# Moving the z projection of a graph attention layer into its edge softmax, with picks in two phases

## The chip, the cores and the metric

The kernel runs on 1 core of a Trainium2 chip. The metric is the device time of one execution in microseconds, as the median over runs. A program of several thousand lines of Python writes every engine's instruction stream by hand, with semaphores between engines.

## The reference

One forward pass over a graph of 3750 nodes with 512 features and 60000 edges sorted by destination: a graph attention layer, an expert-choice mixture of experts, a second graph attention layer and a top-2 mixture of experts, each on a layer norm of x and with x added back. Only the attention layers matter here. Layer 0, with 8 heads of 64:

```
z = einsum('ni,hoi->nho', h, Wfc)
s_src = einsum('nho,ho->nh', z, a_src); s_dst = einsum('nho,ho->nh', z, a_dst)
e = leaky_relu(s_src[src] + s_dst[dst])
ex = exp(e - segment_max(e, dst)[dst])
alpha = ex / segment_sum(ex, dst)[dst]
out = segment_sum(alpha[:, :, None] * z[src], dst)
```

Layer 1 is the same with another slope, e times (1 + et_emb[edge_type]) times the edge weight, and a maximum of at least zero.

## The kernel before, in words

Each attention layer is a stage `front`, which makes z and the edge weights alpha, and a stage `aggregate`, which gathers z rows by edge and sums them. `front` consists of two blocks; a block is one instruction stream for each engine with a barrier of all engines at its end, and `aggregate` starts after another.

**First block, entry.** There are NT = 30 tiles of 128 nodes. SP loads x in five batches of six tiles (`load_x`, L296 to L311) and the weights. VectorE takes statistics of a batch (`stats`, L407), normalises it into two slots (`norm`, L416 to L423) and multiplies the weights with the attention vectors (L431, L432), which gives `wa`. TensorE turns each tile (`turn`, L577), ACT copies it out with two copies (L723, L724) into `edge` and `alpha`, and TensorE makes the scores of source and destination for four tiles at a time (`score`, L585), which it turns back (L598). The scores are split into three bf16 parts (`table`, L449). The scores are also stored to HBM (`src_scores`, L335).

**First block, z.** TensorE projects the 30 tiles with eight matmuls each (L633), ACT copies each out of PSUM (L735), and SP stores it (L358). In layer 0 TensorE also counts, between the tiles, how many edges each node has, from one-hot operands that VectorE makes (L496, L497, L613), and from this come the first edge of each node (L507 to L513). In layer 1 it spreads the edge kinds (L607), which VectorE takes into `wide` (L525).

**First block, picks.** The edges are padded to 61440 and lie in `e` as 16 chunks by 8 heads over the partitions and 15 blocks of 256 edges along the free dimension. Of these blocks, ten get their source scores on TensorE: a pick is 512 edges of one chunk. VectorE makes a one-hot of the key of each edge (L551), TensorE selects with six bf16 matmuls (L674), VectorE masks by tile (L560), and two fp32 matmul records (L683) add the result into one of five PSUM banks. There are 16 x 5 = 80 picks. A row of keys and one of tiles, broadcast to 128 partitions, serves the five picks of a chunk; SP loads them into two slots (`load_rows`, L339). The other five blocks are gathered by POOL, 32 indirect transfers each (`pick`, L373), and turned on TensorE (L664). The destination scores are scattered by POOL to the first edge of each node (L395), read back by ACT in 15 blocks with two transfers each (`load_dst`, L702), turned (L664) and copied out by ACT (L748). TURNS_AT gives the pick before which each block is turned. PICKS_BEFORE gives how many gathered blocks POOL does ahead of its scatters. In layer 0, VectorE also does between picks the counting for the tables of `aggregate` (L472, L475, L476) and the run bounds (`make_bounds`, L458): two compares, two scans, four scalings. At the end come the matmuls of the tables (L690, L691) and ACT's copies of the five sums (L753).

**Second block, edge softmax.** It is a chain on VectorE of five segmented scans over 3840 columns (L787, L803) with passes between them. Each scan needs two small answers of TensorE (L900, L904) to carry over the chunks. ACT makes the flags (L877), the exponentials and the logarithm (L882, L887, L891). Then TensorE turns the weights (L911) and VectorE and ACT copy them into `alpha` (L770). TensorE's stream has nothing else here.

The order on every queue is the order of the program text; nothing is planned at run time.

## Time and profile before

| | |
|---|---|
| runs | 3551.01 us median of 3 (3549.84 to 3555.11) |
| the profiled execution | span 3551.1 us |
| PE busy | 2856.0 us, 80% |
| DVE busy | 2086.8 us, 59% |
| ACT busy | 659.4 us, 19% |
| POOL busy | 1666.6 us, 47% |

The page gives the profiled execution as a span alone. PE is TensorE's matmuls, PEld its weight loads, DVE is VectorE, ACT ScalarE, POOL GpSimd, SP SyncE. A share of the span is an average over stages with different limits, so the stages are read one by one. In the trace, "front_early" and "front_edge" are buffers of the stage `front`, "bank" is PSUM. PEclk is the clock that TensorE was granted, 1.00 being 2.4 GHz. In a timeline row "x8" is the number of instructions merged into it.

### The profile page before, as it was taken

Reading aid. Unit: us, or ns where it says so; the run is one execution under the profiler, and the core shown is the slowest. Engines: PE = TensorE matmul, PEld = TensorE weight load, DVE = VectorE, ACT = ScalarE, POOL = GpSimd, SP = SyncE. Lnnn points to the kernel's source line nnn. Section 1 sums busy time; section 2 is a strip of 40 time slices with the busy share of each in tenths; the row PEclk is TensorE's granted clock in tenths of the full one; section 3 lists DMA queues with packets and bytes.
Section 4 is the critical chain, followed back from the end, with each engine's and each line's share of the span. In section 5 each row is a group of like instructions: output and inputs, shape, how many; then the busy total and the mean of one; then the engine's idle time right before and its main releaser. Section 6 shows DMA issues by size and latency. Waiting matters only on the chain. (4 is left out here: it accounts for less than half of the span.)

```text
span 3551.1 us, 38041 instructions
## 1 busy us (share of the span) xinstructions
PE 2856.0 (80%) x9200; PEld 1383.1 (39%) x9201; DVE 2086.8 (59%) x3517; ACT 659.4 (19%) x1150; POOL 1666.6 (47%) x1601
## 2 busy tenths in 40 slices
PE   5988818888887884299999499990888898784998
PEld 2444402222222553255554244550322223273665
DVE  5778786666665876723332321559666666576554
ACT  2100110000001662011111121001211111161333
POOL 0678007777774000134443137710677777501665
PEclk9999959999998885599999799995999999956999
DMA  4226307777775112045555533720677777545666
GB/s 162 85 89 110 123 5 209 209 209 210 209 209 154 63 66 104 14 115 144 144 145 135 142 83 91 169 90 0 179 210 210 211 211 210 168 178 168 125 125 107
DMA packets 329743, 496.57 MB, mean 140 GB/s; under 512 B 175457, under 2 KB 181073, under 8 KB 328951
## 3 DMA queue, kind: packets, MB, share of 16 engines
q0 software_dynamic: 118528, 313.64, 34.7%
q1 hardware_dynamic: 83367, 176.98, 14.1%
q10 hardware_dynamic: 127696, 4.06, 2.0%
q8 instruction: 79, 1.29, 0.2%
q14 instruction: 73, 0.60, 0.1%
HBM read 407.83 MB, written 86.70 MB: 139 GB/s over the span
## 5 line engine op out<-in xcount | busy, mean ns | idle before, releaser
L994 POOL DMA_INDIRECT aggregate_zg<-z_rows,src_groups x940 | 892.0, 949 | 619.9 <-POOLq L2282 334.1
L1067 PE MATMUL bank<-aggregate_zg,aggregate_onehot 128*128 x1888 | 947.2, 627 | 122.2 <-DVE aggregate_zg L1037 115.5
L1037 DVE TENSOR_TENSOR aggregate_zg<-aggregate_zg,bank 128x1024 f32<-128x1024 f32 x470 | 573.6, 1220 | 429.5 <-DMA aggregate_zg<-z_rows,src_groups 429.1
L1067 PEld LDWEIGHTS bank<-aggregate_zg,aggregate_onehot 128*128 128x128 f32 x1888 | 304.4, 189 | 763.3 <-issue 751.0
L378 POOL DMA_INDIRECT front_d<-src_scores,src_chunks x320 | 325.1, 1016 | 188.4 <-issue 97.2
L1702 POOL DMA_INDIRECT exp_xg<-hn_rows,exp_gather_tok x64 | 71.9, 1123 | 497.1 <-DVE exp_gather_tok L1764 375.7
L674 PE MATMUL bank<-front_w,front_table 128*120 128x512 bf16 x960 | 243.7, 391 | 27.6 <-DVE front_w L551 27.6
L977 ACT ACTIVATE acc<-bank 128x512 f32<-128x512 f32 x60 | 35.8, 597 | 1084.4 <-PE bank L1067 1084.4
L1846 PE MATMUL bank<-exp_w,exp_h_t 128*117 128x512 f32 x512 | 225.7, 595 | 0.7 <-ACT exp_h_t L1793 0.7
L1713 POOL DMA_INDIRECT x_rows<-exp_y,exp_add_tok x64 | 136.5, 2133 | 165.1 <-DVE exp_y L1755 129.8
L1838 PE MATMUL bank<-exp_xg_t,exp_w 128*128 128x468 f32 x512 | 206.1, 561 | 0.7 <-ACT exp_xg_t L1782 0.7
L674 PEld LDWEIGHTS bank<-front_w,front_table 128*120 128x120 bf16 x960 | 130.6, 137 | 175.6 <-issue 94.7
L1015 DVE TENSOR_TENSOR aggregate_onehot<-bank,columns 128x256 f32<-128x256 f32 x472 | 192.1, 416 | 0.0
L683 PE MATMUL bank<-front_z,spread 120*128 120x512 f32 x320 | 168.7, 609 | 0.1
L633 PE MATMUL bank<-front_w,front_edge 128*128 128x512 f32 x360 | 166.7, 599 | 0.0
L1838 PEld LDWEIGHTS bank<-exp_xg_t,exp_w 128*128 128x128 f32 x512 | 98.2, 192 | 107.0 <-issue 107.0
L1754 DVE TENSOR_TENSOR exp_y<-bank,exp_b 117x512 f32<-117x512 f32 x64 | 44.1, 690 | 154.7 <-PE bank L1846 154.7
L1846 PEld LDWEIGHTS bank<-exp_w,exp_h_t 128*117 128x117 f32 x512 | 90.3, 181 | 114.2 <-issue 112.7
L900 PE MATMUL bank<-front_cc,head_sel 128*8 128x32 f32 x20 | 2.8, 231 | 159.4 <-DVE front_cc L789 120.2
L2103 POOL DMA_INDIRECT out_x<-exp_y,exp_slot_rows x66 | 104.5, 1584 | 49.8 <-SPq L2092 20.7
L2097 POOL DMA_INDIRECT exp_xin<-routed_rows,slot_tokens x66 | 64.4, 976 | 124.2 <-DVE exp_x_t L2124 66.8
L2182 PE MATMUL bank<-exp_w,exp_x_t 128*128 x528 | 120.5, 386 | 1.6 <-DVE exp_x_t L2124 1.6
(429 smaller groups left out, 3756.2 us busy)
## 6 DMA issues: line engine op xcount, KB each, us to landing
exp_w<-in_L_ffn_w SPq DMA_DIRECT2D x32, 1024.0 KB, 7.3
z_rows<-front_z SPq DMA_DIRECT2D x60, 256.0 KB, 2.0
aggregate_zg<-z_rows,src_groups POOLq DMA_INDIRECT x940, 3.7
front_early<-src_key SPq DMA_DIRECT2D x16, 640.0 KB, 3.8
front_early<-src_tile SPq DMA_DIRECT2D x16, 640.0 KB, 3.9
front_edge<-src_key SPq DMA_DIRECT2D x16, 640.0 KB, 3.9
front_edge<-src_tile SPq DMA_DIRECT2D x16, 640.0 KB, 4.0
exp_w<-in_L_ffn_W SPq DMA_DIRECT2D x2, 4096.0 KB, 17.4
```

What stands on the lines that cost most here:

```text
L378: pool.indirect_dma_start(picked[:, at:at + H], None, k.src_scores[:, :], bass.IndirectOffsetOnAxis(k.src_chunks[:, n:n + 1], 0)).then_inc ...
L633: mm = nc.tensor.matmul(k.ps[3 + n % 2][:, :], hn_t(c, slice(n * P, (n + 1) * P)), w[:, c, :], start=(c == 0), stop=(c == KC - 1))
L674: mm = nc.tensor.matmul(k.ps[5 + m % 2][0:HT * H, :], parts[:, part, half, :], onehot[:, m % OH, half, :], start=(part == 0 and half == 0) ...
L683: nc.tensor.matmul(sums[b], k.spread[0:HT * H, at:at + P], masked[0:HT * H, (m - 1) % 2, :], start=(c == 0), stop=(c == CH - 1)).then_inc( ...
L994: pool.indirect_dma_start(zg[:, r, j, :], None, k.z_rows[:, :], bass.IndirectOffsetOnAxis(k.src_groups[:, n:n + 1], 0)).then_inc(gathered[ ...
L1015: v.tensor_tensor(onehot_at(n), lanes.unsqueeze(1).to_broadcast([P, J, P]), bcast_last(k.columns[:, n, :], P), ALU.is_equal).then_inc(oneh ...
L1037: v.tensor_tensor(z, z, bcast_last(scales[:, at:at + J * H], DH), ALU.mult).then_inc(msg_ready, 1)
L1067: mm = nc.tensor.matmul(k.banks[:, bass.ds(bank, 1), :].rearrange("p a n -> p (a n)"), onehot_at(n)[:, j, :], zg[:, bass.ds(at, 1), j, :]. ...
L1713: pool.indirect_dma_start(k.x_rows[:, :], bass.IndirectOffsetOnAxis(add_tok[:, u, q:q + 1], 0), y[:, u, q, :], None, compute_op=ALU.add).t ...
L1838: mm = nc.tensor.matmul(k.ps[f][:, 0:CAP], w1[:, u, c, f * P:(f + 1) * P], xg_t[:, c, :], start=(c == 0), stop=(c == KC - 1))
L1846: mm = nc.tensor.matmul(k.ps[4 + q][0:PQ, :], h_t[:, f, q * PQ:(q + 1) * PQ], w2[:, u, f, :], start=(f == 0), stop=(f == F - 1))
L2182: mm = nc.tensor.matmul(k.ps[3 + j][:, 0:DFF1], x_t[:, j, c, :], w1[:, bass.ds(expert[j], 1), c, :].rearrange("p a n -> p (a n)"), start=( ...
```

## The change

It touches the two `front` stages, and `ident`, which gets one more column.

- **z.** Only two tiles (Z0) are projected in the first block. The other 28 are projected in the second: Z_BEFORE gives how many stand ahead of each scan's first answer (2, 5, 4, 5, 3 in layer 0, 2, 7, 3, 5, 3 in layer 1); the rest, nine and eight, stand behind the last answer and ahead of the transposes. There are four PSUM banks and four SBUF slots for them instead of two. ACT copies them between its own operations (`take_upto`), SP stores them.
- **x.** ACT copies each turned tile into `k.x` itself with one copy, and scores and projection read it there. SP loads x a second time in the second block, a batch behind its sixth projected tile; in layer 0 POOL clears the last tile first.
- **Normalised tiles** have four slots. Batch 0 is normalised before the statistics of batch 1, batch 1 before the weight product, and TensorE waits for the product only before the first scores.
- **Picks.** Twelve blocks are picked on TensorE and three gathered. The picks run in two phases of 16 x 3, 96 in all; each chunk's keys and tiles are loaded once in each phase, for three picks. ACT takes the three sums of the first phase in between, before the destination blocks in layer 0.
- **First edges.** Counting by matmul is gone. VectorE counts for each node, against the last destination of each group of 256 edges, the group in which the node starts; POOL gathers that group's row of destinations for each node (30 transfers); VectorE counts inside the row, two tiles a pick. The tables of `aggregate` come from comparisons and four small sets of matmuls between picks (STEPS_AT).
- **Run bounds.** The two scans are replaced by comparisons with the chunk's first and last neighbour.
- **Layer 1.** The kinds are spread between picks 2 and 16 (SPREADS_AT); the run bounds are loaded before the key rows.

The core of the diff:

```diff
-SB = 2 * GE
-TBLK = 5
-HD = D // 2
-GS = GC - 2 * TBLK
+GS = 3
+NB_PE = GC - GS
+PHASES = 2
+WIDE_PICK = 2 * GE
+PB = NB_PE * GE // (PHASES * WIDE_PICK)
+SR = PB * WIDE_PICK
+PICKS = PHASES * CH * PB
+HNS = 4
+ZS = 4
+Z0 = 2
+TURNS_AT = ({**{50 + 3 * n: ("d", n) for n in range(GC - 3)}, 86: ("d", 12), 92: ("d", 13), 94: ("d", 14), 30: ("g", 0), 70: ("g", 1), 89: ("g", 2)},
+            {**{30 + 3 * n: ("d", n) for n in range(GC - 3)}, 70: ("d", 12), 73: ("d", 13), 91: ("d", 14), 47: ("g", 0), 67: ("g", 1), 88: ("g", 2)})
+PICKS_BEFORE = (1, 0)
+STEPS_AT = (18, 20, 23, 26, 29)
+BOUNDS_AT = (33, 36, 39, 42)
+SPREADS_AT = tuple(range(2, 18, 2))
+MODS_AT = tuple(m + 2 for m in SPREADS_AT)
+Z_BEFORE = ((2, 5, 4, 5, 3), (2, 7, 3, 5, 3))
...
+        a_b = early[:, 2 * SR:].bitcast(F32).rearrange("p (a d) -> p a d", a=2)
+        hn = edge[:, 2, SR:SR + HNS * D].rearrange("p (a d) -> p a d", a=HNS)
+        late_rows = edge[:, 2, 0:SR].bitcast(BF16)
+        row_slots = [a.rearrange("p (r n) -> p r n", r=2) for a in (late_rows, early[:, 0:2 * SR])]
+        onehot = k.alpha[:, 0:OH * WIDE_PICK].bitcast(BF16).rearrange("p (u a n) -> p u a n", u=OH, a=2)
         masked = z
-        hn_t = lambda c, at: (k.alpha[:, at] if c == KC - 1 else edge[:, c, at])
+        hn_t = lambda c, tiles: k.x[:, tiles, c * P:(c + 1) * P]
+        z_slots = [edge[:, 2, SR + DR * GE + u * D:SR + DR * GE + (u + 1) * D] for u in range(2)] + [z[:, u, :] for u in range(2)]
...
+        def project(pe, n):
+
+            pe.wait_ge(hn_t_ready, n + 1)
+            if n >= ZS:
+                pe.wait_ge(z_copied, n - ZS + 1)
+            for c in range(KC):
+                mm = nc.tensor.matmul(z_bank(n), k.x[:, n, c * P:(c + 1) * P], w[:, c, :], start=(c == 0), stop=(c == KC - 1))
+            mm.then_inc(z_ready, 1)
+
+        def take_z(act, n):
+
+            act.wait_ge(z_ready, n + 1)
+            if n >= ZS:
+                act.wait_ge(z_stored[n % ZS], 16 * (n // ZS))
+            nc.scalar.copy(z_slots[n % ZS], z_bank(n)).then_inc(z_copied, 1)
+
+        def store_z(sp, n):
+
+            sp.wait_ge(z_copied, n + 1)
+            sp.dma_start(k.z_rows.rearrange("(t p) d -> t p d", p=P)[n], z_slots[n % ZS]).then_inc(z_stored[n % ZS], 16)
...
+                    pool.wait_ge(groups_ready, 1)
+                    for t in range(NT):
+                        pool.indirect_dma_start(edge_rows[:, t, :], None, I["dst_rows"],
+                                                bass.IndirectOffsetOnAxis(group_i[:, t:t + 1], 0)).then_inc(rows_gathered, 16)
...
+                def load_rows(r):
+                    phase, c = r // CH, r % CH
+                    at = slice(phase * SR, (phase + 1) * SR)
+                    if r >= 2:
+                        sp.wait_ge(onehot_ready, (r - 1) * PB)
+                    sp.dma_start(row_slots[r % 2][:, 0, :], keys[c, at].partition_broadcast(P)).then_inc(keys_loaded[r % 2], 16)
+                    if r >= 2:
+                        sp.wait_ge(mask_done, (r - 1) * PB)
+                    sp.dma_start(row_slots[r % 2][:, 1, :], tiles[c, at].partition_broadcast(P)).then_inc(tiles_loaded[r % 2], 16)
...
+                def find_groups():
+                    dve.wait_ge(lasts_loaded, 16)
+                    v.tensor_scalar(corner, k.iota[0:1, :], float(P - 1), None, ALU.is_equal)
+                    chain(v.tensor_copy(lasts, lasts_i))
+                    for t in range(NT):
+                        ins = v.tensor_scalar(less[:, t, 0:NG], lasts, k.node[:, t:t + 1], 0.0, ALU.is_lt, ALU.add, accum_out=group[:, t:t + 1])
+                    chain(ins)
+                    v.tensor_copy(group_i, group).then_inc(groups_ready, 1)
...
+                if layer == 0:
+                    find_groups()
                 stats(0)
+                norm(0)
                 stats(1)
-                norm(0)
+                norm(1)
...
+                def count_inside(t):
+                    if t == 0:
+                        dve.wait_ge(rows_gathered, 16 * NT)
+                    ins = v.tensor_scalar(less[:, t, :], edge_rows[:, t, :], k.node[:, t:t + 1], 0.0, ALU.is_lt, ALU.add, accum_out=inside[:, t:t + 1])
...
+                    if step < 2:
+                        v.tensor_scalar(bounds[:, (TO_FIRST, TO_LAST)[step], :], dst[:, 1:CL + 1], pen[:, step:step + 1], -BIG,
+                                        ALU.not_equal, ALU.mult).then_inc(bounds_ready, 1)
...
+                        other = (0, 2)[step - 2]
+                        out = bounds[:, (PREV, NEXT)[step - 2], :]
+                        chain(v.tensor_tensor(out, dst[:, other:other + CL], dst[:, 1:CL + 1], ALU.not_equal))
+                        v.tensor_scalar(out, out, -BIG, None, ALU.mult).then_inc(bounds_ready, 1)
...
+                    if m == 0:
+                        dve.wait_ge(table_filled, 16)
+                    if m < NT // 2:
+                        for t in (2 * m, 2 * m + 1):
+                            count_inside(t)
+                    if m in STEPS_AT:
+                        (place_first, find_ends, compare_steps, make_tables, take_columns)[STEPS_AT.index(m)]()
+                    if m in BOUNDS_AT:
+                        make_bounds(BOUNDS_AT.index(m))
...
-                root(1)
                 for n in range(NT):
-                    at = slice(n * P, (n + 1) * P)
-                    if n % SBT == 0 and n // SBT + 1 < NT // SBT and n > 0:
+                    if n % SBT == 3 and n // SBT + 1 < NT // SBT:
                         root(n // SBT + 1)
                     act.wait_ge(hn_turned, n + 1)
-                    turned_x = k.ps[n % 2].rearrange("p (c n) -> p c n", c=KC)
-                    nc.scalar.copy(edge[:, :, at], turned_x[:, 0:KC - 1, :])
-                    nc.scalar.copy(k.alpha[:, at], turned_x[:, KC - 1, :]).then_inc(hn_t_ready, 1)
+                    nc.scalar.copy(k.x[:, n, :], k.ps[n % 2]).then_inc(hn_t_ready, 1)
...
+                def take_sums(phase):
+                    for b in range(PB):
+                        act.wait_ge(block_done, ((phase + 1) * CH - 1) * PB + b + 1)
+                        at = (phase * PB + b) * WIDE_PICK
+                        nc.scalar.copy(e[:, at:at + WIDE_PICK], sums[phase * PB + b]).then_inc(sums_taken, 1)
+
+                phase_end = CH * PB
+                halfway = sum(m <= phase_end for m in turns_at)
                 for m, (kind, n) in enumerate(turn_order):
+                    if m == halfway:
+                        take_sums(0)
...
+        projected = lambda n: Z0 + sum(Z_BEFORE[layer][0:n + 1])
...
+                def reload(b):
+                    full = SBT - 1 if layer == 0 and b == NT // SBT - 1 else SBT
+                    sp.dma_start(k.x[:, b * SBT:b * SBT + full, :],
+                                 rows[b * SBT * P:(b * SBT + full) * P, :].rearrange("(t p) d -> p t d", p=P)).then_inc(x_reloaded, 16)
+
+                for b in range(Z0 // SBT):
+                    reload(b)
+                for n in range(Z0, NT):
+                    store_z(sp, n)
+                    if n % SBT == SBT - 1:
+                        reload(n // SBT)
+                if layer == 0:
+                    sp.wait_ge(x_cleared, 1)
+                    sp.dma_start(k.x[0:N - (NT - 1) * P, NT - 1, :], rows[(NT - 1) * P:N, :]).then_inc(x_reloaded, 16)
+                    sp.wait_ge(bounds_stored, 16)
+                sp.wait_ge(x_reloaded, 16 * (NT // SBT + (1 if layer == 0 else 0)))
+                for u in range(ZS):
+                    sp.wait_ge(z_stored[u], 16 * len(range(u, NT, ZS)))
+
+            if layer == 0:
+                @block.gpsimd
+                def _(pool):
+                    pool.wait_ge(z_ready, NT)
+                    nc.gpsimd.memset(k.x[:, NT - 1, :], 0.0).then_inc(x_cleared, 1)
...
+                def take_upto(n):
+                    for t in range(done[0], n):
+                        take_z(act, t)
+                    done[0] = n
+
+                done = [Z0]
                 if layer == 0:
                     act.wait_ge(bounds_ready, 4)
                 else:
                     act.wait_ge(bounds_loaded, 16)
+                    take_upto(projected(0))
                     act.wait_ge(wide_read, 1)
                 for a, kind in enumerate((PREV, TO_FIRST)):
                     ins = nc.scalar.activation(flags[:, a, :], bounds[:, kind, :], ACT.Relu, bias=k.ones[:, 0:1])
                 ins.then_inc(flags_ready, 1)
+                take_upto(projected(2))
                 for n in range(PIECES):
                     at = slice(n * PW, (n + 1) * PW)
                     act.wait_ge(to_act, n + 1)
                     nc.scalar.activation(spread_out[:, at], e[:, at], ACT.Exp).then_inc(from_act, 1)
+                take_upto(projected(4))
...
+                    for t in range(projected(n - 1) if n else Z0, projected(n)):
+                        project(pe, t)
...
+                for t in range(projected(4), NT):
+                    project(pe, t)
+                pe.wait_ge(z_copied, NT)
```

## Rows read from the trace of the kernel before

**Rows 1.** The head of the page: span and instructions.

```profile
span 3551.1 us, 38041 instructions
```

**Rows 2.** Windows: length, busy (x) PE/PEld/DVE/ACT/POOL, PEclk, DMA share, GB/s.

```profile
91.80:216.30 124.50, 118.92 (x726) 58.58 (x725) 94.11 (x90) 17.56 (x30) 89.92 (x94) 0.98 0.32 91
...
216.30:430.00 213.70, 191.54 (x692) 102.52 (x692) 172.54 (x376) 10.42 (x26) 120.02 (x96) 0.94 0.48 116
...
430.00:528.20 98.20, 9.65 (x50) 8.02 (x51) 88.32 (x65) 24.89 (x24) 0.00 (x0) 0.53 0.00 0
...
2198.90:2391.90 193.00, 183.52 (x680) 99.57 (x680) 103.44 (x239) 10.08 (x25) 97.12 (x102) 0.97 0.54 133
...
2391.90:2496.90 105.00, 10.52 (x51) 8.91 (x52) 94.01 (x66) 25.39 (x24) 0.00 (x0) 0.53 0.00 0
```

**Rows 3.** The counting line of before: ns min/median/max, first and last start.

```profile
L472 DVE TENSOR_SCALAR_CACHE_REDUCE alpha<-alpha,front_d x29: 445/451/453, 227.9 to 304.9; 128x234 f32<-128x234 f32 x29
```

**Rows 4.** Timeline, layer 0 entry: start, us, what [idle before <-releaser].

```profile
12.13 3.66 DVE L410 BATCH_NORM_STATS2 front_bn<-x 128x6 f32<-128x512 f32 x6 [7.54 <-DMA x<-in_x]
...
37.34 2.29 DVE L432 TENSOR_REDUCE front_d<-front_d 128x32 f32<-128x2048 f32 x1
...
46.34 4.74 PE L591 MATMUL bank<-front_edge,front_d 128*16 128x512 f32 x6
...
91.84 2.84 PE L633 MATMUL bank<-front_w,front_edge 128*128 128x512 f32 x6
```

**Rows 5.** Windows of L633 alone: length, PE busy (x), PEld busy (x), clock, DMA.

```profile
2085.30:2109.40 24.10, 24.05 (x56) 10.56 (x56) 1.00 0.44 128
```

**Rows 6.** Timeline, layer 1 entry.

```profile
2014.78 3.66 DVE L410 BATCH_NORM_STATS2 front_bn<-x 128x6 f32<-128x512 f32 x6 [3.93 <-DMA x<-x_rows]
...
2039.97 4.62 PE L591 MATMUL bank<-front_edge,front_d 128*16 128x512 f32 x6
```

**Rows 7.** Windows of L683 (two records a pick), selecting matmuls, a turned block.

```profile
2340.00:2383.10 43.10, 20.47 (x40) 7.64 (x40) 1.00 0.24 92
...
2237.30 1.46 PE L674 MATMUL bank<-front_w,front_table 128*120 128x512 bf16 x6
...
2240.75 0.38 PE L664 MATMUL bank<-ident,front_edge 128*128 128x128 f32 x2
```

**Rows 8.** Timeline, long VectorE operations around the picks and TensorE after one.

```profile
222.49 4.15 DVE L461 TENSOR_TENSOR front_edge<-front_wide 128x3840 bf16<-128x3840 int32 x1
...
227.35 2.35 PE L674 MATMUL bank<-front_w,front_table 128*120 128x512 bf16 x6 [2.54 <-DVE front_w L551]
...
307.06 8.15 DVE L467 TENSOR_TENSOR_SCAN front_edge<-front_edge 128x3840 bf16<-128x3840 bf16 x1
...
2088.22 2.21 DVE L519 TENSOR_SCALAR front_e<-front_e,kind 128x3840 f32<-128x3840 int32 x1
```

**Rows 9.** Timeline, first dst blocks of layer 1: issues by ACT, first turn.

```profile
2206.80 15.60 ACTq L704 DMA_DIRECT2D front_edge<-first_scores  x10
...
2212.88 0.44 PE L664 MATMUL bank<-ident,front_edge 128*128 128x128 f32 x2 [1.90 <-DMA front_edge<-first_scores]
```

**Rows 10.** Timeline, softmax of layer 0: a query, last answer, transposes, next stage.

```profile
477.14 0.27 PE L900 MATMUL bank<-front_cc,head_sel 128*8 128x32 f32 x2 [13.19 <-DVE front_cc L789]
...
512.29 0.60 PE L904 MATMUL bank<-front_carry,head_sel_t 8*128 8x16 f32 x2 [0.46 <-DVE front_carry L794]
...
521.17 5.26 PE L911 MATMUL bank<-ident,front_e 128*128 128x128 f32 x30 [8.27 <-ACT front_e L891]
...
528.22 1.05 PE L1050 MATMUL bank<-zero_bf 128*128 128x128 bf16 x16 [1.79 <-PEq L2282]
```

**Rows 11.** Timeline, softmax of layer 1: flags on ACT, last answer.

```profile
2419.67 6.88 ACT L877 ACTIVATE front_wide<-front_edge,ones 128x3840 bf16<-128x3840 bf16 x2 [28.07 <-DVEq L837]
...
2480.02 0.60 PE L904 MATMUL bank<-front_carry,head_sel_t 8*128 8x16 f32 x2 [0.46 <-DVE front_carry L794]
```

**Rows 12.** The key loads, L342 in picks of layer 1.

```profile
DMA to landing us min/median/max: 3.5/3.9/9.5
```

435 lines of the change are left out of this document (201 added, 234 removed).

## The prediction

> **What bounds it now.** The profiled execution spans 3551.1 us [rows 1]; the median of the three runs is 3551.01, so sum and median share one scale. I first cut the trace at the blocks of the two front stages [rows 2]. Each has an entry (layer norm, turns, scores), a z stretch, a pick stretch and the edge softmax. In z and picks TensorE sets the pace (118.92 of 124.50 us and 191.54 of 213.70 in layer 0); in the softmax VectorE does, with 88.32 of 98.20 us, and TensorE is busy for 9.65. So TensorE work can leave the first stretches and lie beside VectorE in the last. What ends a stage is a barrier, so each stage's time counts in full. A measurement of this kernel can tell about 0.2%, 7 us, from no change.
>
> **Entry, layer 0.** The change puts 30 compare-and-count operations before the first statistics. One on 234 columns takes 0.451 us [rows 3], an estimated 0.5 with the read of its sum, so 30 take about 15 us; after a list that lands near 8 they end near 23 us. The statistics could start at 12.13, and the product ended at 39.6 [rows 4]. The normalisation of tiles 0 to 5 follows at 28, then tiles 6 to 11, and the weight product (four operations of 2.29 us) ends near 49.5. The first scores on TensorE waited until 46.34 anyway, for tiles of the second batch; they now start at 49.5: +3.2 us. One copy per turned tile instead of two gives back an estimated 1.4. z begins 1.8 later, at 93.6, and after the two tiles that stay (3.44 us each, eight matmuls, seven tiles in 24.10 [rows 5]) the picks begin at 100.5, not at 216.3. The 30 row gathers that feed the new first edges run on POOL from 23 us; 96 indirect transfers take 120 us there [rows 2], so 30 take 38 and end near 61: hidden, with 33 us in hand.
>
> **Entry, layer 1.** No counting there. Batch 0 is normalised while batch 1 lands (2014.78 [rows 6]), four slots let batch 1 pass without a stop, and the product ends near 2032.9. The scores start there instead of at 2039.97 [rows 6]: -7.1, with the copies -8.5. z starts at 2076.8, picks at 2083.8, not 2198.9.
>
> **Picks.** In a clean stretch 20 picks take 43.10 us, 2.155 each, all of it TensorE [rows 7]. 96 picks take 206.9 us (80 took 172.4). 18 turned blocks of 0.22 add 4 (the pair of transposes took 0.38, overlapping [rows 7]).
> - Layer 1: the eight spreads of the edge kinds move in, 0.9 each, 7 us. I give 3 for row loads. 221 us, so the picks end at 2304.8 and the softmax begins at 2305.8 instead of 2391.9: -86.
> - Layer 0: the table matmuls that stood at the end come inside, 5 us with the small new ones. VectorE has some 0.7 us a pick to spare. The bound scans of 8.15 us leave; two int compares replace them, between 2.2 us (the nearest form, f32 from int32) and 4.15 (the two-tensor compare) [rows 8]; I take 2.2, same scalar form. Two compares of 4.15 with a multiply of about 1.2 remain. Beyond the spare time that is 12 us, at the upper end 16. Small chains add 3, the 30 counts 2. Five idle microseconds cost more than themselves: after 2.5 idle, six matmuls took 2.35 us instead of 1.46 [rows 7, 8]; 4 us for two of them.
> - The dst blocks in layer 0: ACT now first takes the three sums of phase one, after pick 47, and only then issues ten loads; the first block is turned at pick 50, three microseconds later. In layer 1 of before the ten issues held ACT 15.60 us, and the first block was turned 6.1 us after the first issue, TensorE idle 1.90 [rows 9]. Queued behind the issues is ACT's copy of that block, and TensorE's next turn waits for it. Stalls of about 3.3 and 4, and two slow restarts: 9 us, bounds 3 and 18. Row loads 1. Sum 246.7: the picks end at 347.2, the softmax begins at 348 instead of 430: -82.
>
> In both layers POOL has 32 transfers a gathered block, 40 us; three blocks and the 30 scatters end near 262 and 2242 us, before the last of them is asked for.
>
> **Softmax, layer 0.** VectorE's five scans need two answers each from TensorE, and the tiles stand ahead of them in program order: 2, 5, 4, 5, 3, and 9 behind the last answer. Before the third there are 13.1 us between answers [rows 10], and four tiles take 13.8, with a slow restart 15.8; with the first window I put 2 us on VectorE. The last answer went out at 512.3 and settled at 512.9. From there nine tiles take 31 us, where the transposes began 8.3 later (521.17) and closed the block at 528.2, 7.1 further. Now 82.9 - 0.8 (two copies moved off) + 2 + 31 = 115.1 from the block's start; the transposes would end it at 122.9. The last reload of x is issued after the last copy: 0.8, 0.4 to issue, 6.8 to land (the first x load: 5.3 to 12.13 [rows 4]), 1.8 to close: 124.9. Against 98.2 that is +26.7.
>
> **Softmax, layer 1.** Seven tiles stand before the second answer and there are four banks. ACT copies tiles 2 and 3, then waits for `wide_read`, then runs two flag activations, 6.88 us from 2419.67 [rows 11], and only then takes tile 4; tile 8 needs that bank. So TensorE idles until 2427.3 on the old clock, does three tiles (10.3, slow restart 2) and answers at 2439.6 where VectorE asked at 2428.1: +11.5. The last answer (2480.0, 88.7 from the block's start when settled) moves to 100.2; eight tiles 27.5, reload tail 9.8: 137.5 against 105.0, +32.5. No spare time brings it back: VectorE is the chain.
>
> **Sum.** Layer 0: -82 + 26.7 = -55.3. Layer 1: -86 + 32.5 = -53.5. Together -108.8: 3442 us. Aggregation gets the same data; I cost it at nothing, since the block still ends by a barrier after all of z is stored.
>
> Weighed against a rule: between projections TensorE idles for microseconds. In the softmax of before the granted clock was 0.53, that is mostly 1.2 GHz, at 9.65 us busy in 98.2 [rows 2]; in z it was 0.98 to 1.00 [rows 2, 5]. The Trainium skill ("TensorE: Matmul & The Clock Gate", "HAM oscillation") says that each burst after a long enough gap starts at the half clock again. By that every group of tiles would pay about 2 us; where windows have room it is hidden, and the sum would be some 4 us more. The row of the slow restart agrees in kind.
>
> **Rivals.**
> 1. Slower: the low clock persists through the softmax. A tile then takes 6.88 us. 28 tiles are 193 us a layer, TensorE bounds the block, and it lasts about 210 us in layer 0 (+85 on the forecast) and 215 in layer 1 (+77): 3604. It decides from +1.95 us a tile over 56 tiles, a mean clock near 0.64. For it: 0.53 in that window. Against: there was nothing to do there, and six matmuls after a stall were the only slow ones. 4 in 100. The rule of the Trainium skill on bursts ("TensorE: Matmul & The Clock Gate", "HAM oscillation"), read at its worst, is this rival.
> 2. The picks starve. A row now serves three picks instead of five, so each load has about 8 us from slot freed to need. 640 KB landed in 3.9 us median, 9.5 at most [rows 12]; now it is 384 KB. At 9.5 each, 1.5 us on 60 rows: +90, 3532; a part of it, or longer stalls at the dst blocks, gives 3487. 22 in 100.
> 3. The softmax hides all of z: 3442 - 59 = 3383. The nine and eight tiles behind the last answer speak against it. Half of it, if the copies by ACT don't hold up layer 1 or the spare time is better than I count: 3412. 10 in 100.
> 4. The change doesn't do what it says, the freed time coming back at a barrier, because POOL or the first edges are late: 3540 to 3555. 3 in 100.
>
> **Numbers.** Forecast 61 in 100, its own range 3415 to 3472. With the halves of rivals 2 and 3 and the bounds above, 3405 to 3490. Faster by over 0.2%: 0.95; within: 0.01; slower: 0.04.
>
> **What would show it.** Picks from about 100 to 347 us and 2084 to 2305 on a clock shifted by layer 0's gain; 2.155 us a pick; an idle TensorE of some 11 us before its second answer in layer 1; nine and eight projections behind the last answer and block lengths of 125 and 137 us; granted clock above 0.85 in both softmaxes. Wrong if tiles there take over 5 us, if VectorE waits for key loads, or if the last projection is not what the transposes wait for.

## The result, and the profile after

The changed kernel takes 3449.64 us (median of 4 runs, 3447.93 to 3461.61) against 3551.91 for the kernel before on the same chip: ratio 0.972, 95% interval 0.9704 to 0.9737. The forecast was 3442, range 3405 to 3490. The profiled execution spans 3448.6 us, 102.5 less than [rows 1].

The two front stages cut at the same places as [rows 2], picks and softmax of layer 0, then of layer 1 (windows of the changed kernel: length, busy (x) PE, PEld, DVE, ACT, POOL, PEclk, DMA share, GB/s):

```profile
99.50:349.40 249.90, 228.27 (x830) 121.73 (x828) 153.66 (x368) 10.86 (x26) 132.53 (x125) 0.95 0.52 122
349.40:476.40 127.00, 110.07 (x274) 49.57 (x275) 87.64 (x63) 40.74 (x52) 0.52 (x1) 0.94 0.35 119
2037.00:2259.20 222.20, 219.59 (x820) 119.61 (x820) 131.09 (x296) 10.04 (x24) 115.89 (x122) 0.99 0.55 123
2259.20:2396.00 136.80, 107.83 (x275) 48.63 (x276) 94.11 (x66) 40.91 (x52) 0.00 (x0) 0.94 0.34 112
```

See first the softmaxes: TensorE works 110.07 and 107.83 us there, where it worked about 10 [rows 2], and its granted clock is 0.94, where it was 0.53. VectorE's own work hardly changed (88.32 and 94.01 before [rows 2], 87.64 and 94.11 now), and it no longer sets the length. The picks begin at 99.55 instead of 216.3.

Between marks (the first work in the block of the softmax, the first work of the next stage; each good to 0.1 us) the difference of the two traces adds up so, with the prediction's terms beside it:

| stretch | before | after | difference | predicted |
|---|---|---|---|---|
| start to end of picks, layer 0 | 430.06 | 349.47 | -80.6 | -82 |
| softmax, layer 0 | 98.2 | 126.9 | +28.7 | +26.7 |
| from there to the entry of layer 1 | 1471.0 | 1474.1 | +3.1 | 0 |
| entry to end of picks, layer 1 | 392.8 | 308.8 | -84.0 | -86 |
| softmax, layer 1 | 104.9 | 136.6 | +31.7 | +32.5 |
| from there to the end | 1054.2 | 1052.6 | -1.6 | 0 |
| sum | | | -102.7 | -108.8 |

Entry of layer 0 (timeline: start, us, engine, line, operation), the rows that answer to [rows 4]:

```profile
46.55 6.47 PE L647 MATMUL bank<-x,front_d 128*16 128x512 f32 x8 [9.91 <-DVE front_d L494]
...
92.58 7.13 PE L318 MATMUL bank<-front_w,x 128*128 128x512 f32 x16
99.55 0.81 PE L737 MATMUL bank<-alpha,front_table 128*120 128x512 bf16 x3
```

The first scores start only 0.2 us later than before; they now wait for the weight product (VectorE L494). The two tiles of z and the start of the picks came a microsecond earlier than forecast.

First dst blocks of layer 0 (timeline of ScalarE, then the waiting TensorE; answers to [rows 9]):

```profile
231.92 0.59 ACT L801 COPY front_e<-bank 128x512 f32<-128x512 f32 x1 [1.57 <-PE bank L756]
231.93 18.10 ACTq L769 DMA_DIRECT2D front_edge<-first_scores  x10
250.06 0.37 ACT L814 COPY front_d<-bank 128x256 f32<-128x256 f32 x1 [17.56 <-issue]
...
250.58 0.66 PE L725 MATMUL bank<-ident,front_edge 128*128 128x128 f32 x2 [6.28 <-ACT front_d L814]
```

ScalarE takes the third sum, issues ten loads for 18.10 us, and only then copies the first turned block; TensorE waits 6.28 us for that copy (and 2.1 before it for the load).

Softmax of layer 1 (timeline; answers to [rows 11]): VectorE's scan, ScalarE's flags, TensorE behind them.

```profile
2269.38 14.00 PE L318 MATMUL bank<-front_w,x 128*128 128x512 f32 x32
...
2286.80 6.88 ACT L970 ACTIVATE front_wide<-front_edge,ones 128x3840 bf16<-128x3840 bf16 x2 [19.83 <-DVEq L923]
2286.85 8.16 DVE L878 TENSOR_TENSOR_SCAN alpha<-front_edge,front_e 128x3840 f32<-128x3840 bf16 x1
2293.59 1.05 ACT L326 COPY front_edge<-bank 128x512 f32<-128x512 f32 x2
...
2294.29 6.10 PE L318 MATMUL bank<-front_w,x 128*128 128x512 f32 x9 [10.91 <-ACT front_edge L326]
...
2306.76 0.23 PE L998 MATMUL bank<-front_cc,head_sel 128*8 128x32 f32 x2
```

The hole is there: 10.91 us (some 11 were forecast), then nine matmuls in 6.10 us where the full clock needs 3.86. VectorE asked at 2295.3, and TensorE answered at 2306.76.

End of the softmax of layer 0 (timeline; answers to [rows 10]): last answer, tiles, transposes, last loads of x, next stage.

```profile
432.31 0.60 PE L1002 MATMUL bank<-front_carry,head_sel_t 8*128 8x16 f32 x2 [0.46 <-DVE front_carry L885]
432.85 33.74 PE L318 MATMUL bank<-front_w,x 128*128 128x512 f32 x72
...
467.26 3.50 PE L1012 MATMUL bank<-ident,front_e 128*128 128x128 f32 x30 [0.68 <-ACT front_edge L326]
467.60 0.43 SPq L845 DMA_DIRECT2D x<-in_x  x1
468.08 0.46 SPq L856 DMA_DIRECT2D x<-in_x  x1
...
476.40 1.86 PE L1151 MATMUL bank<-zero_bf 128*128 128x128 bf16 x16 [5.64 <-PEq L2384]
```

Nine tiles (72 matmuls) stand behind the last answer, the transposes are done at 470.8, and the next stage starts 5.6 us later, once the last load of x has landed. The six microseconds behind each of the five questions of this block (windows, columns as above):

```profile
358.50:364.50 6.00, 5.54 (x12) 2.52 (x13) 5.20 (x6) 0.00 (x0) 0.00 (x0) 0.72 0.08 29
382.00:388.00 6.00, 6.00 (x12) 2.64 (x12) 5.71 (x4) 0.49 (x1) 0.00 (x0) 0.72 0.00 0
398.00:404.00 6.00, 5.61 (x15) 2.71 (x16) 5.38 (x6) 1.68 (x2) 0.00 (x0) 1.00 0.79 278
417.50:423.50 6.00, 5.54 (x16) 2.68 (x15) 5.30 (x6) 0.59 (x1) 0.00 (x0) 1.00 0.95 299
431.60:437.60 6.00, 5.54 (x10) 2.74 (x11) 4.91 (x9) 2.92 (x4) 0.00 (x0) 0.50 0.00 0
```

TensorE had been idle 1.93, 2.51, 0, 1.17 and 2.69 us before those questions. Behind the three longer gaps the granted clock was 0.72, 0.72 and 0.50, behind the two shorter ones 1.00. In the last window ten matmuls were done instead of sixteen, and nothing hides that one. Layer 1 of the same trace is less tidy: behind gaps of 2.04 and 2.69 us before its first and its last question the clock was 1.00, behind one of 2.69 before the third 0.72.

### The profile page after: what moved, and what is told of

Same layout as the page of the kernel before. It is cut to its first block and busy times, and to the rows that moved or that the text cites. A ratio compares the mean times of both kernels' runs of the same rounds, so it can differ in the third digit from the quotient of the medians.

```text
span 3448.6 us, 37641 instructions
## 1 busy us (share of the span) xinstructions
PE 2910.2 (84%) x8976; PEld 1407.9 (41%) x8977; DVE 2013.8 (58%) x3553; ACT 654.5 (19%) x1088; POOL 1560.9 (45%) x1504
## 5 line engine op out<-in xcount | busy, mean ns | idle before, releaser
L1168 PEld LDWEIGHTS bank<-aggregate_zg,aggregate_onehot 128*128 128x128 f32 x1888 | 312.2, 191 | 751.3 <-issue 739.2
L737 PE MATMUL bank<-alpha,front_table 128*120 128x512 bf16 x1152 | 287.1, 386 | 14.7 <-DVE alpha L618 14.7
L416 POOL DMA_INDIRECT front_d<-src_scores,src_chunks x192 | 195.1, 1016 | 94.6 <-issue 58.2
L737 PEld LDWEIGHTS bank<-alpha,front_table 128*120 128x120 bf16 x1152 | 154.8, 135 | 189.8 <-issue 104.2
L318 PE MATMUL bank<-front_w,x 128*128 128x512 f32 x480 | 219.6, 617 | 12.8 <-ACT front_edge L326 10.9
L756 PE MATMUL bank<-front_z,spread 120*128 120x512 f32 x384 | 200.7, 604 | 0.1
L318 PEld LDWEIGHTS bank<-front_w,x 128*128 128x128 f32 x480 | 93.4, 197 | 129.3 <-issue 129.0
L1939 PEld LDWEIGHTS bank<-exp_xg_t,exp_w 128*128 128x128 f32 x512 | 98.2, 192 | 107.0 <-issue 107.0
L628 DVE SCALAR_TENSOR_TENSOR front_z<-front_edge,half_tile,bank 120x512 f32<-120x512 bf16 x96 | 71.6, 746 | 90.4 <-PE bank L737 90.2
L1168 PE MATMUL bank<-aggregate_zg,alpha 128*128 x224 | 111.3, 622 | 13.8 <-DVE aggregate_zg L1138 12.9
```

What stands on the lines that cost most here:

```text
L318: mm = nc.tensor.matmul(z_bank(n), k.x[:, n, c * P:(c + 1) * P], w[:, c, :], start=(c == 0), stop=(c == KC - 1))
L416: pool.indirect_dma_start(picked[:, at:at + H], None, k.src_scores[:, :], bass.IndirectOffsetOnAxis(k.src_chunks[:, n:n + 1], 0)).then_inc ...
L737: mm = nc.tensor.matmul(k.ps[5 + m % 2][0:HT * H, :], parts[:, part, half, :], onehot[:, m % OH, half, :], start=(part == 0 and half == 0) ...
L756: nc.tensor.matmul(sums[phase * PB + b], k.spread[0:HT * H, at:at + P], masked[0:HT * H, (m - 1) % 2, :], start=(c == 0), stop=(c == CH - ...
L1168: mm = nc.tensor.matmul(k.banks[:, bass.ds(bank, 1), :].rearrange("p a n -> p (a n)"), onehot_at(n)[:, j, :], zg[:, bass.ds(at, 1), j, :]. ...
L1939: mm = nc.tensor.matmul(k.ps[f][:, 0:CAP], w1[:, u, c, f * P:(f + 1) * P], xg_t[:, c, :], start=(c == 0), stop=(c == KC - 1))
```

## The experiments

Nine kernels ran. "The first experiment", here and in the recorded expectations, is the one in which ScalarE takes its copies before the flags. Each kernel's ratio is to the kernel before on its own chip. Blocks are counted from VectorE's first work in the softmax to the first work of the next stage.

**The changed kernel again**, as the yardstick of the experiments.

> The changed kernel itself once more, beside the experiments on the same chip. Expected: 0.972 of the kernel before, as at first (3449.64 to 3551.91); its own two clock-dependent places may move it by some us (the picks of layer 0 ended at 349.5 in its first trace and at 345.1 in two experiments that do not touch them; TensorE ran at a granted clock of 0.50 for 5.7 us behind the last answer of layer 0 in its first trace, and at 1.00 in those experiments).

Measured 3456.59 us (5 runs) against 3555.69: 0.9722 [0.9702, 0.9742]. The softmax of layer 0 was 126.9 us again. That of layer 1 was 139.8, 3.2 more than in the first trace, with the same mark: 64 matmuls behind the last answer in 30.25 us instead of 27.73, and at their start this window:

```profile
2362.00:2364.00 2.00, 2.00 (x3) 0.67 (x2) 2.00 (x3) 1.06 (x2) 0.00 (x0) 0.50 0.00 0
```

So the slow spells (stretches of tiles below the full clock) come and go at a given place from one execution to the next, at up to 3 us each.

A second place varies: from the entry of layer 1 to the end of its picks this trace took 314.5 us, the first 308.8. VectorE waits there for the load of the edge types and then for the first row of keys, and TensorE behind it for its first pick:

```profile
2029.16 0.29 DVE L505 TENSOR_TENSOR front_d<-front_d,chunk_sel 128x128 f32<-128x128 f32 x1 [15.51 <-DMA front_d<-in_et_by_kind]
2039.21 1.28 DVE L618 TENSOR_SCALAR alpha<-front_edge,lanes 128x512 bf16<-128x512 bf16 x4 [5.07 <-DMA front_edge<-src_key]
2040.10 5.34 PE L737 MATMUL bank<-alpha,front_table 128*120 128x512 bf16 x12 [7.18 <-DVE alpha L618]
```

In the first trace the three waits were 10.76, 5.05 and 2.41 us; over all traces with two tiles ahead of the picks that of TensorE lay between 0.56 and 9.04. No experiment moved these loads.

**All of z ahead of the picks again** (the moved projections alone).

```diff
-Z0 = 2
+Z0 = 30
-Z_BEFORE = ((2, 5, 4, 5, 3), (2, 7, 3, 5, 3))
+Z_BEFORE = ((0, 0, 0, 0, 0), (0, 0, 0, 0, 0))
```

> Edit: all 30 tiles of z are projected ahead of the picks again, none in the edge softmax; the rest of the change stays (96 picks in two phases, three gathered blocks, the new first edges, x loaded twice). It tells what the moved projections are worth alone. Theory (the prediction's terms): 28 tiles of 3.43 us go back ahead of the picks in each layer (+96.1), and the softmaxes fall back to about 98 and 105 us from 127 and 137 (-28.7 and -31.7): +131.8 us on the changed kernel, 3581 us, which is some 30 us above the kernel before, since the longer picks (16 more of them, and the first edges inside) cost that much by themselves. Rival A: the other parts of the change cost nothing, and it comes out like the kernel before: 3551. Rival B: a good part of the gain came from the other parts: under 3530.

Measured 3582.54 us against 3555.69: 1.0079 [1.0059, 1.0099], a little slower than before. Windows of its picks in layer 0 and of both softmaxes:

```profile
195.70:445.40 249.70, 229.16 (x828) 122.25 (x828) 153.46 (x368) 10.23 (x25) 103.31 (x94) 0.95 0.51 121
445.40:544.00 98.60, 10.54 (x51) 8.96 (x52) 87.69 (x64) 24.93 (x24) 0.52 (x1) 0.53 0.22 78
2411.30:2516.90 105.60, 10.59 (x51) 9.00 (x52) 94.12 (x66) 25.38 (x24) 0.00 (x0) 0.53 0.21 75
```

The picks of layer 0 take 249.7 us wherever z stands, begin 96.1 us later, and the softmaxes are back at 98.5 and 105.5. The moved projections are worth 126 us (3582.54 less 3456.59; 131.8 were put). All the rest of the change costs 27 us by itself (3582.54 less 3555.69). In the traces 24 us of it lie where the longer picks and the new first edges are: from the start to the end of the picks 445.4 us in layer 0 for 430.1, from the entry to the end of the picks 401.3 in layer 1 for 392.8. Rivals A and B fall.

**Six tiles of z ahead, four fewer behind the last answer.**

```diff
-Z0 = 2
+Z0 = 6
```

> Edit: six tiles of z ahead of the picks instead of two, and four fewer behind VectorE's last answer (five and four are left). Theory: a tile costs its 3.43 us on TensorE before the picks and behind the last answer alike, since in both places nothing else bounds: picks start 13.7 us later, the softmaxes are 13.7 us shorter, 3449 us, within 3 us of the changed kernel. Rival A: the tiles behind the last answer are partly hidden by the chain of exponentials (8.3 us in the kernel before) even with four left: slower by up to 2 x 8 us, 3466. Rival B: the tiles in the softmax are dearer than ahead of the picks (slow clock, copies on ScalarE behind activations): faster by 2 to 4 us a layer, 3443.

Measured 3452.82 us against 3555.69: 0.9708 [0.9684, 0.9732], the same as the yardstick within the interval. The picks of layer 0 ended at 363.79 and of layer 1 at 2272.92, the softmaxes took 110.4 and 126.3 us. Rival A (3466) lies outside the interval. Rival B (3443) lies at its edge, so a tile behind the last answer costs what one ahead of the picks costs to within the few us that these runs tell. The softmax of layer 1 fell by 13.5 from the yardstick's, that of layer 0 by 16.5, for 13.7 us of tiles each; in the latter the second question was followed by no slow spell this time, the fourth and fifth were. Ahead of the softmaxes the gain and loss are less even: the picks of layer 0 ended 17.9 us later, those of layer 1, counted from its entry, only 6.0, as TensorE's wait before the first pick shrank from 7.18 to 0.77 us.

**ScalarE takes its copies before the flags, layer 1.**

```diff
-                    take_upto(projected(0))
+                    take_upto(projected(1))
                     act.wait_ge(wide_read, 1)
```

> Edit: in layer 1, ScalarE takes nine tiles of z instead of two before it waits for VectorE's `wide_read` and runs the two flag activations. Theory: the 10.91 us in which TensorE idles before its third tile of the second window (block of 136.7 us in layer 1) come only from the four full banks behind ScalarE's flags; seven tiles of 3.43 us behind 2269.4 end at 2293.4, VectorE asks at 2295.3, so its answer comes 11.5 us earlier and the block closes 11.5 us earlier. Forecast 3438 us, idle row gone, block 125.2. Rival A: the hole is hidden, because the tiles behind the last answer and the reload of x set the end anyway: 3449, block 136.7. Rival B: the flags, now run behind the ninth tile, come too late for the exponentials: part of the gain, 3444, with VectorE waiting for `flags_ready`.

Measured 3440.16 us against 3556.18: 0.9678 [0.9665, 0.9692]. Its timeline, where the changed kernel had the hole:

```profile
2286.68 0.58 ACT L326 COPY front_z<-bank 128x512 f32<-128x512 f32 x1 [2.85 <-PE bank L318]
2287.16 6.88 ACT L970 ACTIVATE front_wide<-front_edge,ones 128x3840 bf16<-128x3840 bf16 x2
...
2288.29 0.22 PE L998 MATMUL bank<-front_cc,head_sel 128*8 128x32 f32 x2 [1.65 <-DVE front_cc L880]
```

TensorE now waits 1.65 us for VectorE, not VectorE for TensorE. The block of layer 1 fell from 136.6 to 124.9 us: -11.7, the 11.5 of the theory. Both rivals fall: the answer's lateness stood in full on the path.

**dst loads ahead of the sums, layer 0.**

```diff
-                    if m == halfway:
-                        take_sums(0)
                     if (kind, n) == ("d", 0):
                         act.wait_ge(scattered, 16 * NT)
                         for r in range(DR):
                             load_dst(r)
+                    if m == halfway:
+                        take_sums(0)
```

> Edit: in layer 0, ScalarE issues the first ten loads of dst blocks before it takes the three sums of phase one, not behind them. Theory: TensorE waited 6.3 us for ScalarE's copy of the first turned block, which stood behind 18.10 us of issues, and 2.1 us for the load itself, and some 1 us went in the restart; the issues then run at about 200 us beside the picks and all of it goes: 3441 us, picks of layer 0 end 8 to 9 us earlier, both waits gone. Rival A: the picks make it up later, the end of the block being set by loads of rows or the last gathered block: 3449. Rival B: the scatters of the first scores end after pick 47, ScalarE waits for them in front of the sums, and TensorE waits for the sums' banks: no gain or a loss, 3449 to 3455.

Measured 3439.71 us against 3556.18: 0.9676 [0.9663, 0.9689]. Its timeline of ScalarE:

```profile
179.25 19.33 ACTq L769 DMA_DIRECT2D front_edge<-first_scores  x10
227.16 0.59 ACT L801 COPY front_e<-bank 128x512 f32<-128x512 f32 x1 [50.16 <-PE bank L756]
...
235.14 0.37 ACT L814 COPY front_d<-bank 128x256 f32<-128x256 f32 x1 [3.09 <-PE bank L725]
```

The issues run at 179 us beside the picks, both waits of TensorE are gone, and the picks ended at 338.7, against 349.5, 345.9, 345.1, 345.1 and 349.6 in five traces that keep the stall. The stretch varies by itself, and the place is ahead of the stall, between 180 and 220 us. The changed kernel, the first experiment, this kernel, and the four edits together:

```profile
180.00:220.00 40.00, 31.12 (x94) 15.52 (x93) 29.58 (x42) 0.00 (x0) 32.98 (x24) 0.83 0.32 84
```

```profile
180.00:220.00 40.00, 31.11 (x115) 16.15 (x112) 33.05 (x51) 0.00 (x0) 32.99 (x24) 1.00 0.36 95
```

```profile
180.00:220.00 40.00, 31.27 (x94) 15.60 (x93) 29.21 (x42) 0.00 (x0) 32.98 (x24) 0.83 0.61 100
```

```profile
180.00:220.00 40.00, 31.28 (x115) 16.31 (x114) 32.86 (x50) 0.00 (x0) 33.14 (x23) 1.00 0.63 110
```

TensorE waits equally long for VectorE in all four, twice 3.68 us; behind each of these waits six selecting matmuls took 2.8 us in the changed kernel and 1.5 in the first experiment. Like with like, the edit is worth 10.8 us at 0.83 (349.5 to 338.7) and 12.1 at 1.00 (345.1 to 333.0), for a term of 9 with the bounds 3 and 18.

**The last tiles of x loaded one by one.**

```diff
-                    if n % SBT == SBT - 1:
+                    if n % SBT == SBT - 1 and n < NT - 1:
                         reload(n // SBT)
+                    elif n >= NT - SBT and n < NT - 1:
+                        sp.dma_start(k.x[:, n:n + 1, :], rows[n * P:(n + 1) * P, :].rearrange("(t p) d -> p t d", p=P)).then_inc(x_reloaded, 16)
+                    elif n == NT - 1 and layer == 1:
+                        sp.dma_start(k.x[:, n:n + 1, :], rows[n * P:(n + 1) * P, :].rearrange("(t p) d -> p t d", p=P)).then_inc(x_reloaded, 16)
...
-                sp.wait_ge(x_reloaded, 16 * (NT // SBT + (1 if layer == 0 else 0)))
+                sp.wait_ge(x_reloaded, 16 * (NT // SBT - 1 + SBT))
```

> Edit: the last six tiles of x are loaded again one by one, each behind its own projection, instead of in one transfer of 1280 to 1536 KB behind the last. Theory: the transfer issued at 468.08 closes the block of layer 0 (next block's first work at 476.40, though the transposes ended at 470.8), and the one issued at 2386.85 that of layer 1 (2395.96, transposes done at 2390.4). With small transfers the transposes close the blocks some 1.8 us after their end: -3.5 us in each layer, 3442.5 us, blocks 123.5 and 133. Rival A: what closes the block is its fixed cost or the store of the last tile of z: no difference, 3449. Rival B: the added issues on SyncE hold up stores of z: slower by up to 2 us a layer, 3453.

Measured 3454.74 us against 3556.18: 0.9715 [0.9702, 0.9728], in the times no more than the yardstick's spread. In the trace both ends move: the block of layer 0 takes 121.9 us (125.2 in the first of these experiments, whose spells lie at the same questions) and that of layer 1 132.6 (136.6). That is -3.3 and -4.0, as forecast, and the transposes now set the end. The sum of some 7 us is too small for these five runs to show against the other variations; only the traces carry it.

**Windows cut by quarter tiles**, together with the edit on the flags.

```diff
-Z_BEFORE = ((2, 5, 4, 5, 3), (2, 7, 3, 5, 3))
+Z_QUARTERS = ((10, 22, 13, 21, 14), (10, 29, 14, 21, 14))
...
-                    for t in range(projected(n - 1) if n else Z0, projected(n)):
-                        project(pe, t)
+                    for at in range(quarters(n - 1) if n else Z0 * KC, quarters(n)):
+                        project(pe, at // KC, (at % KC,))
```

> Edit: the edit of the first experiment (ScalarE takes nine tiles before the flags in layer 1), and TensorE's windows before VectorE's five questions are cut by quarter tiles (0.86 us) instead of whole tiles: 10, 22, 13, 21, 14 quarters in layer 0 (before 8, 20, 16, 20, 12), 10, 29, 14, 21, 14 in layer 1 (before 8, 28, 12, 20, 12). Theory: only the tiles behind the last answer lengthen the block, at 0.86 us a quarter, and the windows still have 1.9, 2.5, -2.4, 1.2, 2.7 us (layer 0) and about 2, 1.7, 2.7, 1.7, 2.7 us (layer 1) of room: four quarters fewer behind the last answer and the lateness of 2.4 us gone in layer 0, eight fewer in layer 1: -3.4 - 2.4 - 6.9 = -12.7 us below the first experiment, 3425 us. Rival A: TensorE then answers late in several windows and gives it back: 3438. Rival B: the end of the block is set by the reload of x on another clock than the tiles: less than half, 3433.

Measured 3431.39 us against 3556.18: 0.9642 [0.9619, 0.9664]; the first experiment, on the same chip, had 0.9678. The blocks took 121.2 and 118.6 us, against 125.2 and 124.9 of the first experiment: -4.0 and -6.3, 10.3 of the 12.7 expected. The time alone (8.8 us less than the first experiment) would not tell this from rival B, less than half; the blocks do. VectorE's last question of layer 1 was taken up 0.7 us later than with whole tiles (87.0 against 86.3 us from the block's start). The window was not cut too close as such: TensorE had idled 2.51 us before the fourth question, and the 28 matmuls behind it took 13.98 us; in the kernel with the halves, behind a gap of 0.81, they took 12.28 and left 0.97 us.

**The four edits together.** The diffs are those above.

> Edit: the four edits that helped in the traces, together: ScalarE's nine tiles before the flags (layer 1), dst loads issued before the sums of phase one (layer 0), the last tiles of x loaded again one by one, quarter tiles in the windows. Theory: they stand in four different places, so they add up: -11.7 (layer 1's block from 136.6 to 124.9), -8.5 (layer 0's picks), -3.3 and -4.0 (the blocks' ends), -4.0 and -6.3 (quarters): -37.8 us, 3412 us, about 0.961 of the kernel before. Rival: two of them share a path (with small transfers the transposes close the block, and a transfer of z behind them takes their place, or the earlier picks wait for rows): 3422, 0.9635.

Measured 3408.62 us against 3555.69: 0.9601 [0.9579, 0.9622]. The picks of layer 0 ended at 333.0, and the softmaxes took:

```profile
333.00:447.80 114.80, 105.47 (x275) 47.83 (x276) 87.55 (x64) 40.49 (x52) 0.53 (x1) 0.99 0.38 131
2237.60:2352.50 114.90, 105.51 (x274) 47.69 (x274) 94.04 (x65) 40.98 (x52) 0.00 (x0) 0.99 0.40 133
```

TensorE is busy for 105 of 115 us in both, at a clock of 0.99. 48 us less than the yardstick of the same chip (3456.59), where the edits promised 37.8. Between the marks of the two traces the picks of layer 0 gave 13.0 (8.5 expected), their softmax 12.1 (7.3), that of layer 1 24.9 (22.0, plus the spell of 3 in the yardstick). What these stretches gave beyond the sum goes with the clock, as far as the traces show. In the picks the granted clock between 180 and 220 us was 1.00, where the yardstick's was 0.96. In the softmax of layer 0 the gaps before the five questions are now 0.21, 2.49, 0.20, 0.31 and 0.97 us, and the clock falls once, behind the 2.49, where it fell three times in the yardstick. That is not fixed by the gaps: with the same windows the kernel of the quarters had the last 64 matmuls in 29.43 us behind its gap of 0.97, this one in 27.73. The kernel beats both, the one before and the changed one.

**Long comparisons of VectorE in halves**, layer 0, on top of the four.

```diff
-BOUNDS_AT = (33, 36, 39, 42)
+BOUNDS_AT = (33, 36, 39, 42, 44, 47, 50, 52)
...
-                        other = (0, 2)[step - 2]
-                        out = bounds[:, (PREV, NEXT)[step - 2], :]
-                        chain(v.tensor_tensor(out, dst[:, other:other + CL], dst[:, 1:CL + 1], ALU.not_equal))
-                        v.tensor_scalar(out, out, -BIG, None, ALU.mult).then_inc(bounds_ready, 1)
+                        which, part = divmod(step - 2, 3)
+                        other = (0, 2)[which]
+                        out = bounds[:, (PREV, NEXT)[which], :]
+                        if part < 2:
+                            lo, hi = part * CL // 2, (part + 1) * CL // 2
+                            chain(v.tensor_tensor(out[:, lo:hi], dst[:, other + lo:other + hi], dst[:, 1 + lo:1 + hi], ALU.not_equal))
+                        else:
+                            v.tensor_scalar(out, out, -BIG, None, ALU.mult).then_inc(bounds_ready, 1)
```

> Edit: the kernel with all four edits, and in layer 0 each of VectorE's two comparisons of run bounds (4.15 us each between two picks) is made in two halves, behind picks 39, 42, 47 and 50, and the multiply by -BIG (1.16 us) behind picks 44 and 52. Theory: VectorE has some 0.7 us to spare a pick, and the four longest waits of TensorE in the picks of layer 0 (3.68, 3.68, 0.82 and 0.55 us) are what these operations take beyond it. Halves of 2.1 us should cost about 0.55 each, as the whole compare of 2.21 us does, and the multiply nothing: 7.36 us become 2.2 or less, 5 us less in the picks of layer 0 (their end from 333.0 to 328), about 3403 us. Rival A: the lateness of VectorE adds up over the picks however it is cut, since its spare time is used already: no change, 3408. Rival B: TensorE's waits only move, to the dst blocks that begin at pick 50: 2 us or less.

Measured 3406.88 us against 3551.90: 0.9589 [0.9576, 0.9602]. The waits of TensorE in these picks, first of the four edits, then with the halves (engine, line, waited for: us in total, times, longest):

```profile
PE bank L739 <- DVE alpha L620: 12.1, 9, 3.7
```

```profile
PE bank L743 <- DVE alpha L624: 7.3, 11, 2.0
```

-4.8 us of waits, and the picks ended at 329.1 instead of 333.0. That is the price of VectorE's operations beyond its spare time, as the theory has it: each half costs 0.61 to 0.64 us (0.55 were put). The whole time cannot tell 4 us: the two intervals overlap, and in the traces other stretches took the gain back, the softmax of layer 0 with 1.9 us more (a slow spell behind the gap of 0.97) and the wait before the first pick of layer 1:

```profile
2017.63 4.58 PE L743 MATMUL bank<-alpha,front_table 128*120 128x512 bf16 x12 [9.04 <-DVE alpha L624]
```

It was 5.23 us in the kernel of the four edits.

## Why the prediction was right

**Right by its own steps.** The move pays because TensorE's work left stretches that it bounds for one that it did not [rows 2], and the whole forecast (-108.8) came within 6.3 us of the measured -102.5.

- *Entry, layer 0*: +3.2 was forecast, +0.2 measured. The counts stand 0.383 us apart, not 0.5: an operation of 0.46 overlaps the next one, and the read of its sum lies inside. The list was done at 21.0 us, 2 earlier, and the weight product, which the scores wait for, at 46.5 instead of 49.5; the third microsecond lies between the two.
- *Entry, layer 1*: ScalarE's first copy of scores is 7.2 us earlier by the shifted clock (7.1 forecast), the first copy of z 7.6 (8.5).
- *Picks*: 249.9 us in layer 0 to the start of the softmax for the 247.5 forecast (100.5 to 348), 222.2 for 222 in layer 1. (The terms given for layer 0 add up to 246.9, not 246.7.) The int compares took 2.22 and 2.21 us, the two-tensor form 4.15, its multiply 1.16: the lower end of the first bound was right. VectorE's work beyond its spare time held TensorE for 12.3 us in nine waits, where 12 and 5 of small pieces were put, and 4 for slow restarts. The stall at the dst blocks was costed at 9 and showed 6.3 and 2.1 and a slow restart; taking it away gave 10.8 and 12.1, like with like, so it was somewhat mis-sized within its bounds. In layer 1 VectorE waited 5.1 us for one row of keys, behind 10.8 for the edge types, and 2.4 reached TensorE; the prediction gave 3 for all row loads. It did not name the load of the edge types, and other traces show 0.6 to 9.0 us at this place: that 2.4 came so close to 3 is luck.
- *Softmax, layer 0*: the third answer came 2.4 us late (2 forecast), the last was settled 83.4 us from the start (84.1). The block is 2.0 longer than the forecast of 124.9: nine tiles took 33.74 us for the 31 put down, the difference being the spell at half clock behind the last answer. In the first of the edits' traces the spells lay elsewhere and the same tiles took 31.17.
- *Softmax, layer 1*: a hole of 10.91 us, an answer 11.5 late, a block of 136.6 for 137.5. The first experiment settles its cause: with ScalarE's order changed, 11.7 us went.
- *Reload of x as the last to land*: shown by the small transfers, -3.3 and -4.0.

**The rule on bursts.** The rows first: behind the hole of 10.91 us nine matmuls ran 58% longer. Behind VectorE's questions, TensorE's next group of tiles lost 1.6 to 2.9 us or nothing. Counted over all 90 questions of the nine traces that have tiles in the softmax, it lost time behind 28 of 38 idle gaps of 1.78 to 2.69 us, behind 8 of 23 of 0.97 to 1.67, and behind none of 29 shorter ones. One of the eight, the fourth question of layer 0 in the kernel with the dst loads moved, behind a gap of 1.17 us that cost the changed kernel nothing:

```profile
405.00:411.00 6.00, 5.54 (x12) 2.51 (x11) 5.24 (x6) 0.00 (x0) 0.00 (x0) 0.72 0.92 293
```

The prediction priced this for the whole at 4 us beside its sum; in layer 0's softmax it shows as 2.0, and as up to 3 more in layer 1 of the yardstick. The Trainium skill ("TensorE: Matmul & The Clock Gate", "HAM oscillation") expects the half clock behind each gap that is long enough. By that rule, the trace agrees in kind, but not every gap of the same length is followed by it (behind the last one, 2.69 us in each, the clock was 0.50 in the changed kernel and 1.00 in the kernel with ScalarE's copies ahead of the flags).

**The rivals.** The low clock that persists through the softmax is refuted by 0.94 in both windows and by tiles at 3.43 us. Starving picks are refuted by the one wait of 5.1 us. That the softmax hides all of z is refuted by the six-tile kernel: the tiles behind the last answer cost their full time. That the change doesn't do what it says falls with the table above.

**What was missed** is 6 us. By the table 4.6 of it lie in the forecast terms (1.4 and 2.0 in layer 0, 2.0 less 0.8 in layer 1) and 1.5 in the two stretches that were costed at nothing. The larger of these, between the softmax of layer 0 and the entry of layer 1, took 3.1 us longer. In the other traces of changed kernels it took 3 to 7 us longer than before, but 5 us less in the one with all of z ahead. Its code is the same. Up to 650 us into it the traces run level (1167 matmuls before, 1166 in the changed kernel); then they part where the granted clock already varies. The same 50 us in the kernel before, the changed one, and that with the dst loads moved:

```profile
1178.20:1228.20 50.00, 44.36 (x168) 27.65 (x167) 43.10 (x71) 32.13 (x46) 0.00 (x0) 0.86 0.21 79
```

```profile
1126.40:1176.40 50.00, 45.02 (x163) 27.97 (x163) 40.33 (x67) 31.17 (x44) 0.00 (x0) 0.82 0.19 70
```

```profile
1112.80:1162.80 50.00, 45.03 (x158) 28.15 (x157) 40.55 (x68) 31.00 (x44) 0.00 (x0) 0.77 0.18 68
```

TensorE is as busy and does less, at 0.86, 0.82 and 0.77. The stage starts at 528.2, 476.4 and 462.8 us in these three. An earlier start alone does not order them: the six-tile kernel starts it at 474.2, 2 us before the changed one, was granted 0.77, and took 4 us more for it. Why the clock differs there stays open.

## What to carry to other kernels

Work of an engine that bounds one stage can be laid beside another stage's bottleneck, and then the windows between that engine's questions are a budget: count them in units as fine as the work allows, and look at who else stands in line. Windows that left TensorE idle for 0.8 us or less also kept the clock up, in all 29 cases here; a full microsecond already did not always. The largest avoidable costs sat not in TensorE's tiles but in ScalarE, which had its copies queued behind a wait for VectorE (11.7 us) and behind ten DMA issues (11 to 12 us). Measure the enabling parts apart from the moved part: they cost 27 us, and the move earned 126.

## What the runs showed of the hardware

- Idle gaps of only 1.78 to 2.69 us on TensorE were followed by a stretch below the full clock in 28 of 38 cases, gaps of 0.97 to 1.67 us in 8 of 23, shorter ones in none of 29, at 1.6 to 2.9 us lost each time. Behind the same gap the same code lost time in one execution and not in another.
- The same ten DMA issues held ScalarE's queue 15.60 us in layer 1 [rows 9], 18.10 in the changed kernel's layer 0 and 19.33 there when they were issued earlier.
- Thirty compare-and-sum operations of 0.46 us on VectorE, each followed by a read of its sum of 0.08, stood 0.383 us apart.
